# Four layers of cross-attention and feed-forward: the second and third layers' scores as three products of rounded halves

## The reference

```
q, (k, v) = x @ Wq, split(context @ Wkv)
attn = softmax(q k^T / 8)          # layer 2: key mask and clip to [-5, 5] before the softmax
x = x + (attn v) @ Wo + bo
```

## Time and profile before

| | |
|---|---|
| median of three runs | 792.46 us |
| profiled execution, its own time | 791.78 us |
| its span, first to last instruction | 790.5 us |
| mean granted TensorE clock | 0.964 |
| PE busy | 712.0 us (90%) |
| PEld (weight loads) busy | 590.4 us (75%) |
| DVE busy | 532.4 us (67%) |
| ACT busy | 493.1 us (62%) |
| POOL busy | 288.2 us (36%) |

### The profile page before, as it was taken

One profiled execution on the slowest core, in us unless ns is written; L12 is line 12 of the kernel. 1 busy time (PEld: TensorE's weight loads), 2 busy tenths in 40 slices (PEclk: granted clock), 3 DMA queues, 4 the chain that ended last, 5 costly groups with the idle time before them and its releaser, 6 DMA issues.

```text
span 790.5 us, 16493 instructions
## 1 busy us (share of the span) xinstructions
PE 712.0 (90%) x5129; PEld 590.4 (75%) x5129; DVE 532.4 (67%) x1843; ACT 493.1 (62%) x1614; POOL 288.2 (36%) x331
## 2 busy tenths in 40 slices
PE   3999998799979999899998999899999998887597
PEld 1667776588857778779976778788778876776597
DVE  3688887489787988555468988681242067996675
ACT  1888784377679978455565565584544348761375
POOL 0410153557615455425514454520010014353255
PEclk9999997889999999999999999999999999996699
DMA  8887512144272000012140000000000050000221
...
DMA packets 35142, 55.68 MB, mean 70 GB/s; under 512 B 7072, under 2 KB 26400, under 8 KB 33136
## 3 DMA queue, kind: packets, MB, share of 16 engines
...
## 4 chain that ended last, share of the span: by engine, by line
PE 62%; DVE 19%; ACT 7%; issue 5%; POOL 3%; DMA 3%; SPq 0%; DVEq 0%; ACTq 0%; POOLq 0%
PE bank L1141 11%; PE bank L1103 8%; PE bank L1113 8%; PE bank L1033 6%; PE bank L995 6%; PE bank L1009 4%; PE bank L984 3%; DVE s_xn L1322 3%; PE bank L939 3%; DVE s_total L1377 2%; ACT s_S L1854 2%; POOL xs L2055 2%; PE bank L1150 2%; PE bank L962 1%; PE bank L1093 1%
## 5 line engine op out<-in xcount | busy, mean ns | idle before, releaser
L2024 POOL TENSOR_TENSOR s_S<-s_S,s_inv 128x462 f32<-128x462 f32 (+2 forms) x108 | 99.7, 939 | 123.3 <-DVE s_inv L1380 121.8
L995 PE MATMUL bank<-s_A,s_xTq 128*128 128x308 f32 (+1 forms) x256 | 99.6, 493 | 5.1 <-ACT s_S L1872 2.1
L1033 PE MATMUL bank<-s_VW,s_PT 128*128 128x128 f32 (+2 forms) x800 | 98.6, 278 | 4.9 <-DVE s_x L1407 4.8
L1009 PEld LDWEIGHTS bank<-s_ident,s_S 128*128 128x128 f32 x560 | 68.0, 142 | 45.6 <-issue 21.6
L1033 PEld LDWEIGHTS bank<-s_VW,s_PT 128*128 128x128 f32 (+2 forms) x800 | 94.0, 194 | 6.0 <-DVE s_x L1407 5.7
L1886 ACT ACTIVATE s_PT<-bank 128x512 f32<-128x512 f32 (+2 forms) x160 | 84.8, 559 | 19.7 <-PE bank L1009 19.1
L2055 POOL DMA_INDIRECT xs<-s_xn,s_sli x64 | 62.0, 969 | 84.0 <-issue 43.2
L1009 PE MATMUL bank<-s_ident,s_S 128*128 128x128 f32 x560 | 85.8, 276 | 7.2 <-POOL s_S L2024 5.6
L1922 ACT ACTIVATE s_hT<-bank,s_b1T 128x128 f32<-128x128 f32 x184 | 52.3, 370 | 18.7 <-PE bank L1113 16.6
L1854 ACT ACTIVATE s_S<-bank,s_peak 128x77 f32<-128x77 f32 x256 | 58.8, 370 | 5.8 <-DVE s_peak L1343 5.7
L1863 ACT ACTIVATE s_S<-s_S 128x462 f32<-128x462 f32 (+1 forms) x64 | 36.6, 573 | 35.0 <-DVE s_S L1357 29.5
...
## 6 DMA issues: line engine op xcount, KB each, us to landing
...
s_arena<-in_L_w SPq DMA_DIRECT2D x2, 1024.0 KB, 12.0
s_arena<-in_L_h SPq DMA_DIRECT2D x2, 1024.0 KB, 8.8
```

Of the source, the lines that this page charges most:

```text
L995: w = mm(bank[j][:, 0:(g1 - g0) * KEYS], xTq_of(L, n)[:, i % 4, :], A[:, n, g0 * KEYS:g1 * KEYS], start=True, stop=True)
L1009: w = turn(bank[b][:, P * (t - t0):P * (t - t0) + P], S[s][:, P * t:P * t + P], ident)
L1033: w = mm(bank[b][:, 0:P], PT[k][0:m, t, :], VW[0:m, n, t, :], start=t == 0, stop=t == nt - 1)
L2024: p.tensor_tensor(val, val, rep(inv[s][:, h0:h1], KEYS, 2), ALU.mult).then_inc(normed.up(L, i, k), 1)
```

## The change

For the layers in `HALVED` = (1, 2) the scores are formed from rounded halves.

- A new piece `key.L.n.k` (image n, head group k): ACT copies the group's columns of `A` to `key_hi` in float32r; POOL writes `key_lo` = A - key_hi over A. 24 pieces: three of layer 1, image 0, at the end of the first layer's list; three of layer 2, image 0, among the folds; the others among the tiles of the image before.
- `xt.q` of these layers: ACT's copy goes to `xqh` in float32r, at the place of `xTq`, and DVE makes `xql` = transposed rows - xqh; PE frees the bank only behind both.
- `S`: three products for each one, rows high x keys high, rows high x keys low, rows low x keys high, in one PSUM bank. They wait for DVE's and POOL's halves.
- `key_hi` of layer 1 lies in `arena`, of layer 2 in `moe1` and on. So `load.L2w` moves from the second attention to the third (behind the scores of layer 1), and `split.0` to `split.7` wait for the last scores of layer 2.
- `xt.q.1.3` moves one product later, from S.1.10.2 to S.1.11.1.

The diff, cut to its core; the remaining changes of the lists insert the other `key` pieces in the same way (`key.1.2.0` to `key.1.3.1` at S.1.4.2, 5.2, 7.2, 8.2, 9.2; `key.2.1.0` at S.2.1.2, `key.2.1.2` to `key.2.3.2` at S.2.3.2, 5.2, 6.2, 7.2, 9.2, 10.2, 11.2).

```diff
+HALVED = (1, 2)
...
+        key.1.0.0 key.1.0.1 key.1.0.2
...
     S.1.1.1 norm.1.0.0
-    S.1.1.2
+    S.1.1.2 key.1.1.0
     S.1.2.0 load.L2v ln.q.1.1.4 E.1.1.0 E.1.1.1 ln.q.1.1.5 ln.q.1.1.6 ln.q.1.1.7
-    S.1.2.1 E.1.1.2 E.1.2.0 norm.1.0.1 norm.1.1.0 vwb.1.3 load.L2w T.1.0.0 xt.q.1.1 E.1.2.1 T.1.0.1 back.0.2.0
+    S.1.2.1 E.1.1.2 E.1.2.0 norm.1.0.1 norm.1.1.0 vwb.1.3 T.1.0.0 xt.q.1.1 E.1.2.1 T.1.0.1 back.0.2.0
         T.1.0.2
-    S.1.2.2 E.1.2.2 norm.1.1.1
+    S.1.2.2 E.1.2.2 norm.1.1.1 key.1.1.1
     S.1.3.0
-    S.1.3.1
+    S.1.3.1 key.1.1.2
...
-    S.1.10.2 T.1.8.1 norm.1.9.1 E.1.10.2 route.1.0.10 xt.q.1.3
+    S.1.10.2 T.1.8.1 norm.1.9.1 E.1.10.2 route.1.0.10 key.1.3.2
     S.1.11.0 route.1.0.11 load.L2k T.1.8.2 route.1.0.12 O.1.7 send.1.0.0 E.1.11.0 send.1.1.0 add.1.7 send.1.2.0
         stat.1.7 ln.r.1.1.1
-    S.1.11.1 send.1.3.0 ln.r.1.1.2 T.1.9.0 E.1.11.1 norm.1.10.0
+    S.1.11.1 xt.q.1.3 send.1.3.0 ln.r.1.1.2 T.1.9.0 E.1.11.1 norm.1.10.0
...
-        fold.2.0.3 fold.2.0.4 fold.2.0.5 fold.2.0.6 fold.2.0.7 fold.2.0.8 fold.2.0.9 comb.1.0.0 back.1.1.0
+        fold.2.0.3 fold.2.0.4 fold.2.0.5 fold.2.0.6 fold.2.0.7 key.2.0.0 fold.2.0.8 key.2.0.1 fold.2.0.9 comb.1.0.0 back.1.1.0
         ln.q.2.0.0 ln.q.2.0.1 fold.2.0.10 fold.2.0.11 fold.2.0.12 fold.2.0.13 ln.q.2.0.2 ln.q.2.0.3 ln.q.2.0.4
-        ln.q.2.0.5 ln.q.2.0.6 ln.q.2.0.7 fold.2.0.14 fold.2.0.15 comb.1.1.0 ln.q.2.1.0 ln.q.2.1.1 vwt.2.0.0
+        ln.q.2.0.5 ln.q.2.0.6 ln.q.2.0.7 key.2.0.2 fold.2.0.14 fold.2.0.15 comb.1.1.0 ln.q.2.1.0 ln.q.2.1.1 vwt.2.0.0
...
-    S.2.2.2 T.2.0.1 norm.2.1.1 E.2.2.2
-    S.2.3.0 T.2.0.2 E.2.3.0
+    S.2.2.2 T.2.0.1 norm.2.1.1 E.2.2.2 key.2.1.1
+    S.2.3.0 load.L2w T.2.0.2 E.2.3.0
...
     yws = put("yw", [P, YO])
     yw = [yws[:, i:i + 1] for i in range(YO)]
     xq = put("xq", [P, 4, P])
+    at_q = top[0]
     xTq = [put(f"xTq{i}", [P, 4, P]) for i in range(2)]
+    xqh = [put(f"xqh{i}", [P, 4, P], F32R, at=at_q + 2048 * i) for i in range(2)]
+    xql = [put(f"xql{i}", [P, 4, P], F32R) for i in range(2)]
     at_r = top[0]
     xTr = [put(f"xTr{i}", [P, 4, P]) for i in range(2)]
     at_m = top[0]
     moe1 = put("moe1", [P, 4096])
     moe2 = put("moe2", [P, 4096])
     at_v = top[0] + 4 * 4096
+    at_a = top[0]
     arena = put("arena", [P, 5632])
     V0 = put("V0", [P, NB, 12, 32], at=at_v)
     at_w = top[0]
...
     GM = put("GM", [P, 4, 512])
     XQ = [put(f"XQ{i}", [P, 4, 4, P], at=top[0] + 8192 * i) for i in range(2)]
     VW = put("VW", [P, NB, 10, P])
+    at_A = top[0]
     A = put("A", [P, NB, 16 * KEYS])
+    key_lo = put("key_lo", [P, NB, 16 * KEYS], F32R, at=at_A)
+    one = 4 * 16 * KEYS
+    key_hi = {(L, n): put(f"key_hi{L}{n}", [P, HEADS[L] * KEYS], F32R, at=o)
+              for n in range(NB) for L, o in ((1, at_a + (4 * 4096 if n == 0 else one * (n - 1))),
+                                              (2, at_m + one * n), (3, at_A + one * n + one // 2)) if L in HALVED}
     at_s = top[0]
     S = [put(f"S{i}", [P, C0]) for i in range(3)]
     PT = [put(f"PT{i}", [P, 10, P]) for i in range(2)]
...
     filled, vbd_made = signal("filled", "init"), signal("vbd_made", "vbd")
     normed = signal("normed", ((L, i, k) for L, i, part in events("norm") for k in part_of(L, part)
                                if not norm_on_dve(L, i, k)))
+    hi_made, lo_made = signal("hi_made", "key"), signal("lo_made", "key")
+    q_lo = signal("q_lo", (a for a in events("xt") if a[0] == "q" and a[1] in HALVED))
     xb_made, vwb_made = signal("xb_made", "xb"), signal("vwb_made", "vwb")
     x_ffn = signal("x_ffn", "down")
     split_lo = signal("split_lo", "split")
...
                 for t in range(t1 - t0):
                     w = turn(bank[b][:, P * t:P * t + P], xn[:, t0 + t, 0:P], ident)
                 w.then_inc(xt_sum.up(u, L, g), 1)
+                if u == "q" and L in HALVED:
+                    drained[b] = q_lo.at(u, L, g)
                 empty[b] = row_lo.at(u, L, g) if (u, L) == ("r", 2) else xt_made.at(u, L, g)
             elif kind == "wq":
                 g, = at
...
                     continue
                 b, (h0, h1) = bank_s[piece], GROUPS[L][k]
                 pe.wait_ge(*xt_made.at("q", L, n))
-                pe.wait_ge(*key_ready(L, n))
-                w = None
+                if L in HALVED:
+                    pe.wait_ge(*q_lo.at("q", L, n))
+                    pe.wait_ge(*lo_made.at(L, n, k))
+                else:
+                    pe.wait_ge(*key_ready(L, n))
+                q, w = use["xTq", ("q", L, n)] % 2, None
                 for j, g0, g1 in score_banks(L, b, h0, h1):
                     free(j)
-                    w = mm(bank[j][:, 0:(g1 - g0) * KEYS], xTq_of(L, n)[:, i % 4, :], A[:, n, g0 * KEYS:g1 * KEYS],
-                           start=True, stop=True)
+                    out, cols = bank[j][:, 0:(g1 - g0) * KEYS], slice(g0 * KEYS, g1 * KEYS)
+                    if L in HALVED:
+                        hi, lo = key_hi[L, n][:, cols], key_lo[:, n, cols]
+                        mm(out, xqh[q][:, i % 4, :], hi, start=True, stop=False)
+                        mm(out, xqh[q][:, i % 4, :], lo, start=False, stop=False)
+                        w = mm(out, xql[q][:, i % 4, :], hi, start=False, stop=True)
+                    else:
+                        w = mm(out, xTq[q][:, i % 4, :], A[:, n, cols], start=True, stop=True)
                     empty[j] = s_left(L, i, k)
                 w.then_inc(scores.up(L, i, k), 1)
             elif kind == "T":
...
                 dve.wait_ge(*xt_made.at(*at))
                 v.tensor_tensor(flat(xl[g]), bank[bank_t[piece]], flat(xh[g]).bitcast(F32),
                                 ALU.subtract).then_inc(row_lo.up(*at), 1)
+            elif kind == "xt" and at[0] == "q" and at[1] in HALVED:
+                u, L, g = at
+                q = use["xTq", (u, L, g)] % 2
+                dve.wait_ge(*xt_made.at(u, L, g))
+                v.tensor_tensor(flat(xql[q]), bank[bank_t[piece]], flat(xqh[q]).bitcast(F32),
+                                ALU.subtract).then_inc(q_lo.up(u, L, g), 1)
             elif kind == "up":
                 g, o = at
                 n = ffn_n["up", g, o]
...
                         if g:
                             act.wait_ge(*wq_sum.at(g - 1))
                     else:
-                        dst = xTq_of(L, g)
+                        dst = (xqh if L in HALVED else xTq)[use["xTq", (u, L, g)] % 2]
                         act.wait_ge(*q_room(L, g))
                 else:
                     dst = xTr_of(L, g)
...
                 t0, t1 = tiles(u, L, g)
                 a(flat(dst)[:, 0:P * (t1 - t0)], bank[bank_t[piece]][:, 0:P * (t1 - t0)],
                   ACT.Copy).then_inc(xt_made.up(u, L, g), 1)
+            elif kind == "key":
+                L, n, k = at
+                cols = slice(GROUPS[L][k][0] * KEYS, GROUPS[L][k][1] * KEYS)
+                act.wait_ge(*fold_act.at(L, 1, HEADS[L] - 1))
+                if (L, n) == (1, 0):
+                    act.wait_ge(*att_sum.at(0, NT - 1))
+                elif L < 3:
+                    act.wait_ge(*up_made.at(L - 1, BLOCKS[L - 1] - 1))
+                    act.wait_ge(*d_sum.at(L - 1, BLOCKS[L - 1] - 1))
+                a(key_hi[L, n][:, cols], A[:, n, cols], ACT.Copy).then_inc(hi_made.up(L, n, k), 1)
             elif kind == "wq":
                 g, = at
                 act.wait_ge(*wq_sum.at(g))
...
                 act.wait_ge(*loaded("L2w"))
                 if n < 8:
                     act.wait_ge(*d_sum.at(1, BLOCKS[1] - 1))
+                    act.wait_ge(*scores.at(2, NT - 1, last_score(2)))
                 else:
                     act.wait_ge(*gates.at(1, last_of(1)))
                 hi, _, src = dense(n)
...
                     val = S[s][:, h0 * KEYS:h1 * KEYS].rearrange("p (h k) -> p h k", k=KEYS)
                     p.tensor_tensor(val, val, rep(inv[s][:, h0:h1], KEYS, 2),
                                     ALU.mult).then_inc(normed.up(L, i, k), 1)
+            elif kind == "key":
+                L, n, k = at
+                cols = slice(GROUPS[L][k][0] * KEYS, GROUPS[L][k][1] * KEYS)
+                pool.wait_ge(*hi_made.at(L, n, k))
+                p.tensor_tensor(key_lo[:, n, cols], A[:, n, cols], key_hi[L, n][:, cols].bitcast(F32),
+                                ALU.subtract).then_inc(lo_made.up(L, n, k), 1)
             elif kind == "xb":
                 g, = at
                 pool.wait_ge(*loaded("const"))
...
                     L, v = int(name[1]), 1 if name[2] == "k" else 0
                     sp.wait_ge(*prod_sum.at(L - 1, v, 1))
                 elif name == "L2w":
-                    sp.wait_ge(*d_sum.at(0, BLOCKS[0] - 1))
+                    sp.wait_ge(*scores.at(1, NT - 1, last_score(1)))
                 elif name == "L3b":
                     sp.wait_ge(*y_made.at(1, BLOCKS[1] - 1))
                     sp.wait_ge(*ht_made.at(1, BLOCKS[1] - 1))

```

26 lines of the change are left out of this document (13 added, 13 removed).

## The result

The changed kernel takes 802.61 us (median of four runs, 801.27 to 804.22) against 791.89 (790.46 to 792.75) for the kernel before on the same chip: ratio 1.0138, interval 1.0113 to 1.0163. It is slower by about 11 us; 787.4 was forecast, and the range to 793.5 misses it.

What follows compares the result with a forecast made beforehand. PE was taken to bound both attentions, ScalarE the second after the change. Gains of 0.9 us (second layer) and 4.2 (third), 5.1 in sum, gave 786.7 for the profiled execution, 787.4 us for the median; range 780.5 to 793.5.

Steps and rivals of the forecast that it cites:

- PE's saving: Scores in both halved attentions: 1.66 us a tile instead of 2.09, 0.43 less, 13.8 us if PE alone decided.
- The next engines' margin: Both attentions: next engine 0.46 and 0.58 us behind PE; third layer's pace 5.39 us, with 0.20 distance.
- VectorE's 0.17 us a tile: Rows' subtraction on VectorE in each halved layer: 0.69 us an image, 0.17 us a tile.
- GpSimd's pieces at nothing: Key subtractions on GpSimd, 3.2 us an image, costed at nothing; uncovered, up to 1.2 us at each of 18 pieces.
- ScalarE's copies: Key high halves: 1.6 us an image, 0.4 us a tile; 0.7 us lost in the second attention's start.
- The rule on shared ports: VectorE's scaling waits for GpSimd's instructions: some 0.5 us a layer, gain 4 us instead of 5; left out.
- Second layer, start: Second attention's start: 0.8 us lost to the rows' subtraction and handover, 0.7 to image 1's key copies.
- The moved load and return: Dense weights' load moved to the third attention, returned rows behind it: costed at nothing.
- The slow rival: ScalarE bounds the second attention at nine key pieces: second layer loses 8 us, third gains 4.2, 796; chance 8%.
- the forecast's 4.2 us gain: Third attention: 4.5 us gained over 16 tiles, less 0.3 for the first image's key copies.

Runs made afterwards that it cites:

- e11: Third layer alone halved, with VectorE's third-layer sums taken over 19 of 77 keys: 788.18 us, ratio 0.9939 to the kernel before.
- e10: The kernel before, with VectorE's third-layer sums taken over 19 of 77 keys: 788.41 us, ratio 0.9965.
- e3: Changed kernel without VectorE's rows' subtractions and with image 0's key halves serving all images (18 of 24 key pieces gone): 789.28 us, ratio 0.9960.
- e13: The kernel before, without ScalarE's row sums of the second layer's exponentials from the fourth tile on: 793.47 us, ratio 1.0016.
- e18: Second layer alone halved, its peaks over 19 of 77 keys and no ScalarE row sums from the fourth tile on: ratio 1.0003 to the kernel before.
- e1: Changed kernel without VectorE's eight subtractions for the rows, the third product taking the rows' high half: 794.52 us, ratio 1.0040.
- e7: Changed kernel with VectorE's rows' subtraction as a piece of its own, in most groups some score products behind the transposes: 802.05 us, ratio 1.0124.
- e12: Changed kernel with all ScalarE key copies, but GpSimd's key subtraction for image 0 alone: 800.47 us, ratio 1.0105.
- e2: Changed kernel with image 0's key halves serving all images, 18 of 24 key copies and subtractions gone: 794.76 us, ratio 1.0035.
- e5: The kernel before with only the dense weights' load moved to the third attention: 791.86 us, ratio 0.9998.
- e6: Third layer alone halved, the load left as in the kernel before: 794.63 us, ratio 1.0042.

## Why the prediction was wrong, step by step

**PE's saving: right.** Three products of a 462-column score in e11 against one in e10, between the same neighbours (timeline of PE; starts):

```profile
436.59 2.40 PE L1033 MATMUL bank<-s_VW,s_PT 128*128 128x128 f32 x20
438.82 0.94 PE L995 MATMUL bank<-s_A,s_xTq 128*128 128x462 f32 x2
439.60 0.49 PE L1009 MATMUL bank<-s_ident,s_S 128*128 128x128 f32 x3
439.93 0.69 PE L995 MATMUL bank<-s_A,s_xTq 128*128 128x308 f32 x2
```

```profile
437.83 2.40 PE L1058 MATMUL bank<-s_VW,s_PT 128*128 128x128 f32 x20
439.99 0.46 PE L1017 MATMUL bank<-s_key_hi,s_xqh 128*128 128x462 f32 x1
440.28 0.37 PE L1018 MATMUL bank<-s_key_lo,s_xqh 128*128 128x462 f32 x1
440.49 0.37 PE L1019 MATMUL bank<-s_key_hi,s_xql 128*128 128x462 f32 x1
440.70 0.49 PE L1034 MATMUL bank<-s_ident,s_S 128*128 128x128 f32 x3
440.95 0.39 PE L1017 MATMUL bank<-s_key_hi,s_xqh 128*128 128x308 f32 x1
```

The spacing inside is 0.29, 0.21, 0.21, in sum 0.71 against 0.78, which looks like a saving of only 0.07. But the value products and the transposes ahead of a rounded product are 0.07 and 0.08 shorter (2.16 for 2.23, 0.25 for 0.33). From value products to the second score it is 3.12 us against 3.34: 0.22, of which 0.08 is the second score's own early start, so 0.14 a score. A tile thus saves about 0.4 (0.43 forecast), and the light tiles above show 0.36 to 0.39. The proportion to columns holds (0.21 for 462, 0.14 for 308).

**The next engines' margin: the step that failed.** The prediction set PE's saving against the *average* busy time of VectorE (5.02 us a tile) and a distance of 0.20. Averages hide that VectorE's and ScalarE's work is uneven over the four tiles of an image. Even with next to nothing added (e3), the third attention's pace is 60.63 / 11 = 5.51, worse than the 5.39 forecast with all of it added; the one tile that grew to 7.29 is 0.76 us of those 60.63. With everything added the pace is 5.84, so eleven tiles take 5.0 us more than forecast: 1.3 of it is there in e3, and 3.7 is the price of the side work, the next terms. That VectorE holds the pace is shown by e11 (5.30 a tile with VectorE lighter, e10 5.56). In the second layer two engines share that part (e13 to e18).

**VectorE's 0.17 us a tile: mis-sized.** It stood at 5.5 us over two layers plus a hold without a price. Measured: 5.5 of work, 7.6 of VectorE waiting in front of it, and 8 us of the whole time (e1). Row had shown 1.47 us of idle in front of the third attention's first group; for the groups inside an attention there was no such room. Timeline of ScalarE, VectorE and PE, second group of the third attention: VectorE, 90% busy, stands idle for 1.80 us, and the first score 1.01.

```profile
431.56 0.59 ACT L1864 ACTIVATE s_xqh<-bank 128x512 fp32r<-128x512 f32 x1
432.18 0.69 DVE L1667 TENSOR_TENSOR s_xql<-bank,s_xqh 128x512 fp32r<-128x512 f32 x1 [1.80 <-ACT s_xqh L1864]
...
432.97 0.45 PE L1018 MATMUL bank<-s_key_hi,s_xqh 128*128 128x462 f32 x1 [1.01 <-ACT s_xqh L1864]
```

e7 speaks against this wait as the whole price: nearly without it the kernel is as slow. How the 8 us divide between work and wait stays open.

**GpSimd's pieces at nothing: wrong, by about 2 us** (e12), and not by the way that the prediction had weighed. It had set PE's waits for late normalisations against the plan's spacing, and those waits did double in the third attention (418 to 510). Waits by engine and line, kernel before, then after (total us, times, longest):

```profile
PE bank L1009 <- POOL s_S L2024: 2.9, 4, 1.2
```

```profile
PE bank L1035 <- POOL s_S L2067: 5.8, 8, 1.6
```

But e12, without the pieces, has the same 5.8 us in 8 places, so they are not what doubled the waits. What the pieces cost is the next term, VectorE's time. ScalarE's copies were priced at 0.7 us in the second layer's start and at 0.4 us a tile of ScalarE's time; by the difference of e2 and e12 (794.76 and 800.47) they cost 5.7 us over both layers.

**The rule on shared ports: right, its size too small, and left out of the sum.** VectorE's scaling got 4.6 us longer in sum, where 0.5 us a layer was worked out. e12 takes that back (20.8 + 25.5 = 46.3 us of scaling, 46.6 before, 51.2 after), and in the third attention alone 1.7 us of VectorE's time with 1.7 us of the stage. The sum of the scaling moves with other things too: e3, without those pieces, has 49.0. In the changed kernel the addition of a return, 0.67 us in the earlier trace rows, takes 1.34 us as a key piece runs on GpSimd beside it. The Trainium skill (SBUF — State Buffer, section "Who interferes with whom") has a VectorE instruction with two SBUF inputs, as this addition is, contend with a GpSimd instruction that reads SBUF. The trace agrees:

```profile
434.26 2.70 POOL L2067 TENSOR_TENSOR s_S<-s_S,s_inv 128x462 f32<-128x462 f32 x3 [1.58 <-DVE s_inv L1406]
436.91 0.84 POOL L2073 TENSOR_TENSOR s_key_lo<-s_A,s_key_hi 128x308 fp32r<-128x308 f32 x1
```

```profile
436.96 1.34 DVE L1656 TENSOR_TENSOR s_x<-s_x,s_yb 128x512 f32<-128x512 f32 x1
```

**Second layer, start.** Forecast 0.8 + 0.7 late; it is 2.73 at O.0. The first score is 1.05 late (PE's wait in front of it grew from 0.43 to 1.17, the 0.8 of the forecast), and from there to O.0 it takes 16.05 us instead of 14.37, where 0.7 was forecast. This part is the additions': without either it takes 14.23 (e3), with the key pieces alone 15.97 (e1), with the subtractions and image 0's keys alone 15.60 (e2). Timeline, against the earlier trace rows:

```profile
227.04 0.58 ACT L1864 ACTIVATE s_xqh<-bank 128x512 fp32r<-128x512 f32 x1
227.65 0.69 DVE L1667 TENSOR_TENSOR s_xql<-bank,s_xqh 128x512 fp32r<-128x512 f32 x1
...
228.44 0.45 PE L1018 MATMUL bank<-s_key_hi,s_xqh 128*128 128x462 f32 x1 [1.17 <-DVE s_xql L1667]
```

**The moved load and return: right.** e5 is at 0.9998; the late return's addition waited for nothing (the 436.96 row).

**The slow rival** had the place right, the second attention with its key pieces behind a full ScalarE (ScalarE's copies: the 5.7 us above), but gave the third layer the forecast's 4.2 us gain where e6 shows a loss of 3.3. Those 7.5 us are more than its distance from the measured time (802.6 less 796). Its mechanism, ScalarE alone, is half of what the runs show: with ScalarE light the second layer's halves still cost 0.52%.
